# Attention maxima from 32-row tiles, two heads side by side in the array

## The reference

```
q, k, v = x @ Wq + bq, x @ Wk + bk, x @ Wv + bv        # 16 heads of 8
scores  = q k^T / sqrt(8) + rel_bias[bucket(k_pos - q_pos)]
context = softmax(scores) @ v
```

## Time and profile before

| | |
|---|---|
| median of three runs | 3968.6 us |
| the profiled execution | 3982.96 us |
| its span | 3981.1 us |
| mean granted TensorE clock | 0.937 |
| TensorE busy | 3413.4 us (86%) |
| VectorE busy | 2896.5 us (73%) |
| ScalarE busy | 1895.8 us (48%) |
| GpSimd busy | 1550.2 us (39%) |

### The profile page before, as it was taken

One profiled execution on the slowest core, in us unless ns is written; L12 is line 12 of the kernel. 1 busy time (PEld: TensorE's weight loads), 2 busy tenths in 40 slices (PEclk: granted clock), 3 DMA queues, 4 the chain that ended last, 5 costly groups with the idle time before them and its releaser, 6 DMA issues. The chain is left out here.

```text
span 3981.1 us, 60519 instructions
## 1 busy us (share of the span) xinstructions
PE 3413.4 (86%) x21021; PEld 2120.6 (53%) x21076; DVE 2896.5 (73%) x6400; ACT 1895.8 (48%) x3447; POOL 1550.2 (39%) x1015
## 2 busy tenths in 40 slices
PE   5999999878999984677748888888886999999987
PEld 3667776556777763344423333333333666666653
DVE  7888888556777755433239899999997777777765
ACT  2555556324566540222237676676663333333325
POOL 2311111541222100588847877877874011111112
PEclk9999999989999985799879999999998999999999
DMA  6433332004444423233332232222322222222211
GB/s 151 94 90 89 88 88 54 1 13 111 101 98 100 105 60 113 58 43 44 43 81 76 84 103 87 87 76 70 96 78 57 90 88 87 87 87 88 88 59 43
DMA packets 242528, 314.18 MB, mean 79 GB/s; under 512 B 46450, under 2 KB 157779, under 8 KB 231588
## 3 DMA queue, kind: packets, MB, share of 16 engines
q1 hardware_dynamic: 208308, 289.02, 26.7%
q0 software_dynamic: 22528, 17.32, 3.3%
q10 hardware_dynamic: 11392, 3.97, 0.5%
HBM read 251.93 MB, written 57.08 MB: 78 GB/s over the span
## 5 line engine op out<-in xcount | busy, mean ns | idle before, releaser
L574 DVE TENSOR_REDUCE a_Mx<-a_Sx 128x2 f32<-128x512 f32 (+1 forms) x1024 | 590.1, 617 | 173.7 <-PE a_Sx L626 127.6
L2187 POOL TENSOR_TENSOR a_inp<-a_dtu,a_Bs 128x1024 f32<-128x1024 f32 x256 | 598.5, 2361 | 168.8 <-DMA a_Bs<-a_brows 159.0
L2465 DVE TENSOR_TENSOR_SCAN a_h<-a_dA,a_inp 128x1024 f32<-128x1024 f32 x256 | 583.2, 2284 | 39.6 <-ACT a_dA L2348 22.5
L2591 PE MATMUL a_Y<-a_hc,g_ident 128*128 128x512 f32 x1024 | 493.9, 606 | 8.8 <-DVE a_hc L2477 5.9
L347 POOL TENSOR_TENSOR a_rest<-a_qk,a_parts 128x512 f32<-128x512 f32 x64 | 75.3, 1177 | 917.9 <-ACT a_parts L399 917.9
L413 ACT ACTIVATE a_Pr<-a_SA 128x512 f32<-128x512 f32 x512 | 305.1, 596 | 167.4 <-DVE a_SA L524 79.2
L623 PE MATMUL a_Sx<-att_Kp,att_Qp 96*128 96x256 bf16 (+1 forms) x2048 | 346.5, 262 | 42.2 <-DMA att_Qp<-a_crows 18.1
L2348 ACT ACTIVATE a_dA<-a_dtA,a_A 128x512 f32<-128x512 f32 x512 | 329.9, 681 | 97.2 <-DVE a_h L2465 95.5
L1937 ACT ACTIVATE f_sg<-f_GB 128x512 f32<-128x512 f32 x272 | 162.7, 598 | 436.0 <-PE f_GB L2013 435.9
L2063 PEld LDWEIGHTS f_OUT<-g_routed_wd,f_hm 128*128 128x128 f32 x2176 | 280.6, 191 | 124.2 <-issue 90.4
L2591 PEld LDWEIGHTS a_Y<-a_hc,g_ident 128*128 128x128 f32 x1024 | 198.5, 196 | 238.1 <-issue 227.5
(11 more groups left out here) (473 smaller groups left out, 6788.0 us busy)
## 6 DMA issues: line engine op xcount, KB each, us to landing
a_Bs<-a_brows SPq DMA_DIRECT2D x256, 256.0 KB, 3.3
f_Cs<-f_crows SPq DMA_DIRECT2D x512, 128.0 KB, 2.9
att_Qp<-a_packing SPq DMA_DIRECT2D x192, 192.0 KB
att_Kp<-a_packing SPq DMA_DIRECT2D x192, 192.0 KB
a_packing<-a_parts SPq DMA_DIRECT2D x64, 384.0 KB
a_packing<-a_parts SPq DMA_DIRECT2D x64, 128.0 KB
a_Cs<-a_brows SPq DMA_DIRECT2D x32, 256.0 KB, 3.8
g_x<-x SPq DMA_DIRECT2D x8, 512.0 KB, 7.4
```

The lines of the kernel that those rows point to most:

```text
L574: nc.vector.tensor_reduce(Mx[(k + 2 - (j < LATE)) % 2][:, t, 2 * jj:2 * jj + 2], Sx[t][:, 0:2 * wd].rearrange("p (h q) -> p h q", h=2), AX ...
L2187: nc.gpsimd.tensor_tensor(inp[n % Q][:], dtu[k][:], Bs[n % Q][:].unsqueeze(1).to_broadcast([P, CH, GT]), ALU.mult).then_inc(s["mulB"], 1)
L2465: nc.vector.tensor_tensor_scan(h[n % 2][:].rearrange("p c q -> p (c q)"), dA[m % 2][:].rearrange("p c q -> p (c q)"), inp[n % Q][:].rearra ...
L2591: nc.tensor.matmul(Y[c][:], ident[:], hc[n % Q][:, c], start=False, stop=(n == N - 1))\
```

## The change

The maxima no longer use the 96 rows of `Qp` and `Kp`, but tiles of their own. `Qm` and `Km` (two buffers each, 128 partitions, 4 heads, 256 columns) hold four groups of four heads, one in each 32 partitions: 24 rows of products of parts (three parts-products of 8 rows), 6 bias rows, 2 rows of zeros. A step now does one query tile t for four heads: in both of its rounds u, a matmul on the 32 rows of one group into `Sx[0]` and one on the 32 rows of the next group into `Sx[1]`; then a full-array matmul for the bias or the mask in each bank. TensorE waits once a step, for all reductions before. The steps of a half are the same in number; t is 0 in even steps and 1 in odd ones.

The tiles are filled by 16 transfers a batch on the sync queue, of 8 or 16 rows of 2 KB, before the six reads of `Qp` and `Kp`. They wait for the maxima of the batch two before. TensorE's maxima wait for them (`mpk`) and no longer for `packed`, which is awaited in the turn of the scores. GpSimd's last split operation waits for both. The ones in `Km` come from a new constant (two transfers of 256 KB at the start), the bias rows of `Qm` from eight transfers a start, and VectorE clears two (second attention: four) tiles. The parts of the bias lines (`lparts`) now lie in `bexp`, so `place` waits for the stored rows before it loads `bexp`.

```diff
@@ attention, block.sync
+                def rows_of_maxima(k):
+                    sp.wait_ge(bias.crows_stored, NPART * 16)
+                    for r in range(4):
+                        sp.dma_start(Qm[k][32 * r + 24:32 * r + 30], bias.crows[:, 4 * r:4 * r + 4]).then_inc(s["m_rows"], 16)
...
+                    for k in range(2):
+                        sp.dma_start(Km[k][:], w["kmrows"]).then_inc(s["m_consts"], 16)
...
                         if m:
                             wait(sp, s["mpacked"], 16 * (b + 2))
+                        if b == -3:
+                            sp.wait_ge(s["m_cleared"], 4 if causal else 2)
+                            if not causal:
+                                sp.wait_ge(s["m_consts"], 32)
+                        wait(sp, s["mx_mm"], 16 * (b + 2))
+                        mb = (b + 3) % 2
+                        for r in range(4):
+                            hs = slice(4 * r, 4 * r + 4)
+                            for dst, at, lo, hi in ((Qm, 0, 0, 2), (Qm, 16, 0, 1), (Km, 0, NPART, NPART + 1),
+                                                    (Km, 8, NPART, NPART + 2)):
+                                to = 32 * r + at
+                                sp.dma_start(dst[mb][to:to + DH * (hi - lo)],
+                                             dram[lo:hi, :, hs].rearrange("n e h q -> (n e) h q")).then_inc(s["mpk"], 16)
...
                         bias.store(sp)
+                        rows_of_maxima(0)
+                        rows_of_maxima(1)
@@ block.gpsimd
                     wait(g, s["packed"], 6 * 16 * bb)
+                    wait(g, s["mpk"], 16 * 16 * bb)
@@ block.vector
+                for tile in (*Qm, *Km) if causal else Qm:
+                    nc.vector.memset(tile[:].rearrange("p h q -> p (h q)").bitcast(F32), 0.0).then_inc(s["m_cleared"], 1)
...
-                            for t in range(TB):
-                                wait(v, s["mx_mm"], 16 * bb + (2 * jj + t + 1))
-                                wd = P * (t + 1) if causal else S
+                            q, t = divmod(jj, 2)
+                            wd = P * (t + 1) if causal else S
+                            for e in range(2):
+                                wait(v, s["mx_mm"], 16 * bb + (2 * jj + e + 1))
@@ block.tensor
-                def maxima(b, kb, j):
-                    for t in range(TB):
-                        n = 16 * b + 2 * j + t
-                        wait(pe, s["red_done"], n - 1)
-                        wd = P * (t + 1) if causal else S
-                        both = Sx[t][:, 0:2 * wd].rearrange("p (u q) -> p u q", u=2)
-                        for u in range(2):
-                            h = 2 * j + u
-                            nc.tensor.matmul(both[:, u], Qp[kb][0:KM, h, t * P:t * P + P], Kp[kb][0:KM, h, 0:wd],
-                                             start=(u == 0), stop=False)
+                def maxima(b, j):
+
+                    q, t = divmod(j, 2)
+                    wd = P * (t + 1) if causal else S
+                    wait(pe, s["red_done"], 16 * b + 2 * j)
+                    both = [Sx[e][:, 0:2 * wd].rearrange("p (u q) -> p u q", u=2) for e in range(2)]
+                    for u in range(2):
+                        for e in range(2):
+                            rows = slice(32 * (2 * (q // 2) + e), 32 * (2 * (q // 2) + e) + 32)
+                            nc.tensor.matmul(both[e][:, u], Qm[b % 2][rows, 2 * (q % 2) + u, t * P:t * P + P],
+                                             Km[b % 2][rows, 2 * (q % 2) + u, 0:wd], start=(u == 0), stop=False)
+                    for e in range(2):
+                        first = 8 * (q // 2) + 4 * e + 2 * (q % 2)
...
                     if c:
+                        wait(pe, s["packed"], 6 * 16 * (b + 1))
...
                         if x_ and j == LATE:
-                            wait(pe, s["packed"], 6 * 16 * (b + 3))
+                            wait(pe, s["mpk"], 16 * 16 * (b + 3))
@@ BiasSetup
-        self.lparts = sc.sb("lparts", [H, NPART, 3 * N], BF16)
+        self.lparts = bexp[0:H].rearrange("p i h q -> p (i h q)")[:, 0:NPART * 3 * N].rearrange("p (i n) -> p i n", i=NPART)
...
+        eng.wait_ge(self.crows_stored, self.NPART * 16)
         for i in range(self.NPART):
             eng.dma_start(self.bexp[:, i], bass.AP(self.lines.tensor, i * H * 3 * N + S - P,
```

More of the change, by code:

```diff
@@ L150, in attention @@
     scale = 1.0 / math.sqrt(DH)
-    CROW, MROW, KM = 3 * 3 * DH, 96, 96
+    CROW, MROW = 3 * 3 * DH, 96
     NPART, BUF, NP = ATT_PARTS, ATT_BUF, 8
@@ L169, in attention @@
         Qp, Kp, V = held["Qp"], held["Kp"], held["V"]
+        Qm, Km = ([sc.sb(f"{n}{i}", [P, 4, S], BF16) for i in range(2)] for n in ("Qm", "Km"))
         Mx = [sc.sb(f"Mx{i}", [P, TB, H]) for i in range(2)]
@@ L613, in _ @@
                 pe.wait_ge(w_in, W_ALL)
-                def maxima(b, kb, j):
-                    for t in range(TB):
-                        n = 16 * b + 2 * j + t
-                        wait(pe, s["red_done"], n - 1)
-                        wd = P * (t + 1) if causal else S
-                        both = Sx[t][:, 0:2 * wd].rearrange("p (u q) -> p u q", u=2)
-                        for u in range(2):
-                            h = 2 * j + u
-                            nc.tensor.matmul(both[:, u], Qp[kb][0:KM, h, t * P:t * P + P], Kp[kb][0:KM, h, 0:wd],
-                                             start=(u == 0), stop=False)
+                def maxima(b, j):
[10 more added lines that the diff above has]
+                        first = 8 * (q // 2) + 4 * e + 2 * (q % 2)
                         if causal:
-                            last = nc.tensor.matmul(both[:, :, wd - P:wd], identb[:],
+                            last = nc.tensor.matmul(both[e][:, :, wd - P:wd], identb[:],
                                                     maskq[:].unsqueeze(1).to_broadcast([P, 2, P]), start=False, stop=True)
@@ L629, in maxima @@
                             lo, hi = (0, P) if t == 0 else (FROM, S)
-                            last = nc.tensor.matmul(both[:, :, lo:hi], flip[:],
-                                                    bmax[:, 2 * j:2 * j + 2, P * (1 - t) + lo - FROM:P * (1 - t) + hi - FROM],
+                            last = nc.tensor.matmul(both[e][:, :, lo:hi], flip[:],
+                                                    bmax[:, first:first + 2, P * (1 - t) + lo - FROM:P * (1 - t) + hi - FROM],
                                                     start=False, stop=True)
@@ L699, in step @@
                     bb = b + 3
+                    if b == 0:
+                        pe.wait_ge(s["consts"], (BUF if causal else 6) * 16)
                     if not causal and b == 0:
@@ L736, in step @@
                         if b == -2 and j == LATE:
-                            pe.wait_ge(s["consts"], (BUF if causal else 6) * 16)
-                            if not causal:
+                            if causal:
+                                pe.wait_ge(s["m_cleared"], 4)
+                            else:
+                                pe.wait_ge(s["m_rows"], 8 * 16)
                                 pe.wait_ge(bias.placed, 16)
@@ L758, in step @@
                         if x_ and j == LATE:
-                            wait(pe, s["packed"], 6 * 16 * (b + 3))
+                            wait(pe, s["mpk"], 16 * 16 * (b + 3))
                         if (x_ if j >= LATE else m):
-                            maxima(slot(b, j)[0], (k + 2 - (j < LATE)) % BUF, slot(b, j)[1])
+                            maxima(*slot(b, j))
                         if a and j == 5:
@@ L2624, in l0_attn @@
                               "rel": a["L0_attn_rel_bias"], "hot": a["c_hot"], "flip": a["c_flip"],
[L2625 removed]
+                              "krows": a["c_krows"], "kmrows": a["c_kmrows"], "up": a["L0_up"], "down": a["L0_down"]}, False, res["held"])
 def l1_attn(nc, res, a):
```

11 lines of the change are left out of this document (7 added, 4 removed).

## The result

The changed kernel takes 4124.5 us (median of 4 runs, 4121.65 to 4127.77) against 3967.9: a ratio of 1.0388, interval 1.0376 to 1.0401. It is 157 us slower; 51 were forecast. The direction was right, the forecast size was a third of what came.

What follows compares the result with a forecast made beforehand. TensorE, busy 97 us of 100 in both attentions, was taken as the bound, with VectorE (89) also near its limit in the first. 13+33+5 = +51 us on 3968.6 gives 4020, range 3960 to 4075.

Steps and rivals of the forecast that it cites:

- part 3: Transfers on the sync queue: 16 more issues take 4.8 us, loop 17.1 under the new 18.3, hidden, cost 0.
- rival B: Sync queue becomes the loop in the second attention: 18.9 or 20.1 us a batch, 4038 or 4076; chance 0.11.
- Parts 1 and 2: Matmuls of the maxima and their wait for reductions: +0.42 us a batch in first attention, +1.04 in second.
- The changes of tiling: Passages between whole-array and tiled matmuls in the maxima: value matmuls show 0.10 us in, 0.11 out; 0.20 taken together.
- the stall of step 4: First attention: TensorE waits 0.4 us for VectorE's reductions of step 3 before the maxima of step 4.
- the late and uneven pairs: Second attention, step 7: reductions start later and their pair is 0.27 us longer, part of +0.96 at the transpose.
- Rival A: Tiled and full matmuls of the maxima follow each other without a gap, changes free: 3969 us; chance 0.17.
- C: Both attentions: array's time counts, the wait doesn't bite as VectorE's work fills gaps: -69 us, 3900; chance 0.10.
- D: The pairs of 32-row matmuls don't run together: 97 us beside the 51, about 4100; chance 0.05.
- Part 4: Start: look-up lines stored 4.8 us later, behind the first batch's loads, delaying bexp, for which TensorE waits: +4.8 us.

Runs made afterwards that it cites:

- relax: The changed kernel, but GpSimd's last split operation waits for the reads of the batch two before, not of the batch before; 4033.6 us, ratio 1.0167.
- half: The changed kernel with 8 of the 16 transfers of a batch (third and fourth group of heads not loaded); 4026.4 us, ratio 1.0153.
- order: The kernel before with only the new order and one wait a step for all earlier reductions, 96-row matmuls, no new transfers; 4041.1 us, ratio 1.0183.
- order_fine: The kernel order, but each bank waits only for the reductions before the last one, as before the change; 3980.4 us, ratio 1.0028.
- one_group: The kernel relax with both matmuls of a pair on the same 32 rows, so they can't run side by side; 4107.7 us, ratio 1.0343.
- early_store: The kernel relax with the bias lines stored before the first batch's 22 reads, not behind them; one run, 4038.4 us.

## Why the prediction was wrong

**The step that failed is part 3**: "I take 0.30, so 4.8 us [...] = 17.1, under the new 18.3 [...] Cost 0". The loop was found and written down with all its members, and each of its terms but one was taken too short:

```
                             forecast   upper bound named   one loop   mean of 28
write, until read               3.2           4.4             4.04        3.65
16 issues                       4.8           6.6             5.98        6.27
six reads landed                7.9            -              9.26        9.67
split, next write               1.2           1.2             1.18        1.18
loop                           17.1          20.1            20.46       20.76
```

Three terms made it. The issues were priced by the 2-row constants and not by the reads that stand next to them in the same queue; they are 0.37 apart (5.98/16), nearly the latter's 0.40. The landing was read off the DMA share as the moment it falls to 0.05, but what the waiting engine sees is later: here the share is 0.53 in the window from 1232 and 0.11 from 1233, and GpSimd starts at 1234.33. And the write was taken at 3.2, which is the shortest that occurs (3.22), with a mean of 3.65. Its upper bound of 4.4 was no landing time: in the kernel before, the reads wait for the row of the maximum, in the changed kernel for the write. The sync queue's own waits of 1100 to 1300 us, before and after:

```profile
SPq L26 <- DMA att_Qp<-a_mrow: 40.1, 12, 3.4
```

```profile
SPq L302 <- DMA a_packing<-a_parts: 23.2, 9, 3.9
```

A margin of 1.2 us on a loop with four terms of that kind was no cover. With my own upper bounds the loop was 20.1, and this stood there as rival B with a chance of 0.11; at 20.76 it came out above even that end, since the landing had been given no bound.

**Rival B was the truth in the second attention, and its price too low.** It gave 4076 at most. The batches average 20.84, which is the mean of the loop; single ones vary with its terms (18.7 to 22.8 in a row of batches). (20.84-17.30) x 32 = 113, beside 118.6 by the stages. In the first attention, which B left at its forecast, the loop closes as well: its 19 loops from 202.8 to 594.8 us average 20.63, and GpSimd waits 3.5 to 6.8 us in each. There TensorE and VectorE alone need 20.27 (relax), so it adds only 0.2 us a batch (20.49).

**Parts 1 and 2 were right for the even batches.** Taken without the loop, as relax and half show, the batches are 20.27 and 18.27; the forecast was 20.1 and 18.3. The changes of tiling cost 0.12 and 0.10 (forecast 0.10, 0.11), the stall of step 4 is 0.36 (0.4). The working by single steps was good to 0.15 us a batch. It was off in how it divides. In the first attention the wait alone costs 0.70 and the tiles give 0.14 back, 0.56 in all where 0.42 was forecast. In the second I charged the +1.04 mostly to the late and uneven pairs, and order and order_fine divide it into 0.74 for the wait, 0.38 for the order, and -0.15 for the tiles. What the sum lacked even without the loop is the batches that are not even: it took 32 equal ones, and relax is 66 us above before where 51 were forecast.

**Rival A** (free changes) falls by the timeline, **C** by order: the array's time is not what counts once the wait is there, and **D** by one_group.

**Part 4** was near in size (3.8 for 4.8) by luck and wrong in its mechanism, as early_store shows. TensorE no longer waits for bexp; it waits 22.9 us for the bias rows of `Qm`, whose transfers the forecast had not charged, and half of the 3.8 us is the new order and wait. The bexp matmuls start at 69.09, not near 72.

The sum by the runs: loop 91 (after less relax), wait 46 and what it costs at the start and in uneven batches 15, order 12, the rest of the start 1 (83.4 against order's 82.0), tiles -9: 156 of 157. The terms are differences of kernels whose runs spread over 6 us or more, so the small shares are rough.

## What to carry to other kernels

When a change adds transfers to a queue, close the loop before calling them hidden: from the write through every issue to the landing, to whoever waits for it, and back to the write. Compare its length with the stage's period, with every term at its longer bound; here the loop passed by 1.2 us in forecast and failed by 2.5. And a wait that protects a buffer should name the batch that used that buffer: waiting for one batch more cost nothing for as long as the queue was short, and 91 us afterwards.

Running small matmuls side by side helps only where the array is what is waited for. Here two banks had to be filled and emptied together for it, which took away the overlap of TensorE and VectorE (46 us in even batches), and each passage between tiled and full-array work cost half of what the two pairs between had saved.

## What was not expected of the hardware

- Two 32-row tiles in different banks do run fully side by side: four matmuls of 256 columns in 0.22 us (0.43 on one group of rows).
- A change between 32-row tiles and the full array costs 0.10 to 0.12 us, the same as between the full array and 32-column tiles (0.10 and 0.11).
- A transfer of 16 or 8 rows (32 or 16 KB) takes the sync queue 0.37 us in the mean, nearly as long as one of 192 KB (0.40). The small transfers saved bytes, and what the loop counts here is issues.
- The waiting engine is released later than the DMA share falls: the share is 0.11 in the window from 1233 us, GpSimd starts at 1234.33.
